# Five stages on one core: tiles shared across stages, inputs loaded a stage ahead, constants in order of need

## The chip, the cores and the metric

The kernel runs on one core of a Trainium2 chip. The metric is the device time of one execution in microseconds (us). The core's engines are TensorE (PE, with its weight loads PEld), VectorE (DVE), ScalarE (ACT), GpSimd (POOL) and SyncE (SP). They run side by side and wait for each other by semaphores. Transfers (DMAs) are issued here by SP, ACT and POOL.

## What is computed

The reference applies two layers to `x` of shape (4, 512, 256). Each layer is an attention and a feed-forward part, each followed by a residual sum and a normalisation:

```python
x = _layernorm(x + _L0_attn_ref(x, ...))   # softmax attention, global and windowed, 16 heads
x = _layernorm(x + _L0_ffn_ref(x, ...))    # 8 routed experts (2 chosen) and a shared one
x = _layernorm(x + _L1_attn_ref(x, ...))   # gated delta rule, 12 heads of 128 keys and 32 values
x = _layernorm(x + _L1_ffn_ref(x, ...))    # 16 routed experts (4 chosen, 128 places each) and a shared one
```

The constants of the kernel (the identity for transposes, masks, triangular matrices, tables for counting) are further inputs.

## The kernel before, in words

`whole_program` (L2663) calls five functions one after the other; each is a stage:

- `layer0_attention` (names `a_`): 4 batches of 512 tokens. For each, PE transposes `x`, projects queries, keys and values, finds the row maxima, scores, weighs and projects out; DVE adds `x` and normalises; POOL stores the result `x1` to HBM.
- `layer0_experts` (`f_`): for each batch, PE transposes `x`, routes, and runs ten hidden units (`hide`) and nine sums (`project`); ACT applies gelu, DVE adds up and normalises, POOL stores `x2`.
- `layer1_projections` (`p_`): gates, decays and values of all tokens. The results that the next stage keeps in SBUF lie in the object `kept` (`hT`, `decays`, `beta`); the gates, the values `v` and the decays `alpha` are stored to HBM by SP.
- `layer1_delta_rule` (`d_`): 12 heads, pipelined. Per head PE projects keys and queries, DVE convolves them, POOL inverts small triangular blocks by substitution, PE and DVE run the recurrence over four chunks, and SP stores the head's output `o_out` to HBM.
- `layer1_output` (`m_`): projects the heads' outputs (`project`), adds `x2`, normalises, routes, runs the shared expert, and then gathers rows for each of 16 experts, multiplies, and scatters them back with addition; a last normalisation makes the output.

A stage allocates its own SBUF tiles, PSUM banks and semaphores, and writes one program for each engine in a `Block`. Each engine works its list in order, waits included. The stage ends when all engines are through their lists; the lists end in waits for the last stores to land (`stored`), as in L475 on POOL:

```python
pool.dma_start(x1_b[b, :, :, :], x1[:]).then_inc(stored, 16)
pool.wait_ge(stored, 16 * BATCH)
```

Then the semaphores are cleared and all engines meet (`clear_and_free_semaphores`, `all_engine_barrier`), and the next stage starts with its loads. What is at the head of each stage:

- Attention: SP issues eleven loads of constants and weights (L151), all counted on one semaphore `loaded`, then `x` of the first two batches (L155). PE, ACT and DVE wait for all eleven (`loaded`, 176) before their first instruction; PE's first work is `turn_x(0)` (L168).
- Experts: SP loads `ident`, `x` of batch 0, the gate's weights (PE and ACT wait for the first and third as `first_in`), then the experts' weights `w1` (L704, L709) with the biases, `w2`, and further `x`. `turn_x(0)` is L727, `hide` is L751; ACT waits for all of `w1` before its first gelu (L816).
- Projections: SP loads `ident`, `x`, the gates' weights, small vectors, the values' weights, and at the end the first two heads' weights for the next stage. `turn_x(0)` is L1060. At the stage's end SP stores `alpha` and the last values (L1036) and waits for both to land.
- Delta rule: POOL fills `U32`, `L32` and `X2` with zeros and three small tiles with constants; PE, ACT and DVE wait for all six (`consts`, 6). SP loads decays, values and gates. PE's first work is `project` (L1468). The last head's output is multiplied by DVE (`finish`, L1934), stored by SP (L1422), and awaited.
- Output: SP loads `ident`, `w_o`, `o` and `x2` of two batches. ACT first issues nine loads (L2293), two stores of zeros (L2296) and two loads of the router's weights, turned, one element at a time (L2299); only then it copies PE's transposes (`project`, L2306). PE transposes `o` in L2124 and projects it in L2133.

## Time and profile before

| | |
|---|---|
| median of 3 runs | 1870.4 us (1864.61 to 1874.24) |
| the profiled execution, its own time | 1870.46 us |
| its span, first to last instruction | 1868.5 us |
| mean granted clock of TensorE | 0.915 of full speed |
| PE, DVE, ACT, POOL busy | 79%, 56%, 35%, 35% of the span |

The stages can be told apart in the timeline by the prefixes of the tiles' names: attention to about 549 us, experts to 737, projections to 823, the delta rule to 1602, the output to the end. A row of the timeline gives the start, the duration, the engine, the line, the operation and the tiles, and in brackets how long the engine had been idle and what it was released by. "SPq" and "ACTq" are issues of transfers, which take time on the issuing engine; the landing is later.

### The profile page before, as it was taken

Reading aid. Unit: us, or ns where it says so; the run is one execution under the profiler, and the core shown is the slowest. Engines: PE = TensorE matmul, PEld = TensorE weight load, DVE = VectorE, ACT = ScalarE, POOL = GpSimd, SP = SyncE. Lnnn points to the kernel's source line nnn. Section 1 sums busy time; section 2 is a strip of 40 time slices with the busy share of each in tenths; the row PEclk is TensorE's granted clock in tenths of the full one; section 3 lists DMA queues with packets and bytes.
Section 4 is the critical chain, followed back from the end, with each engine's and each line's share of the span. In section 5 each row is a group of like instructions: output and inputs, shape, how many; then the busy total and the mean of one; then the engine's idle time right before and its main releaser. Section 6 shows DMA issues by size and latency. Waiting matters only on the chain. (4 is left out here: it accounts for less than half of the span.)

```text
span 1868.5 us, 27548 instructions
## 1 busy us (share of the span) xinstructions
PE 1483.0 (79%) x10473; PEld 1005.7 (54%) x10524; DVE 1054.7 (56%) x2369; ACT 661.6 (35%) x1308; POOL 645.1 (35%) x1037
## 2 busy tenths in 40 slices
PE   4787787786959996857599999999999997387782
PEld 3354554444536664523367666576666686365572
DVE  3846556547123444558477767777777732155553
ACT  3062161341512220534254444554455522022112
POOL 3020020200000000012686666877667762111343
PEclk8999899899979998979799999999999976598897
DMA  1000000000012001341213432223432121421355
GB/s 55 1 1 1 23 2 1 23 1 1 12 39 65 23 12 57 118 121 39 43 34 67 80 80 55 46 60 80 80 75 45 38 43 29 128 97 57 86 118 140
DMA packets 223876, 97.08 MB, mean 52 GB/s; under 512 B 166905, under 2 KB 212386, under 8 KB 223746
## 3 DMA queue, kind: packets, MB, share of 16 engines
q1 hardware_dynamic: 212306, 80.88, 18.1%
q0 software_dynamic: 5376, 12.59, 2.6%
q10 hardware_dynamic: 6064, 1.86, 0.4%
q8 instruction: 83, 1.36, 0.3%
q14 instruction: 47, 0.39, 0.1%
HBM read 63.48 MB, written 31.82 MB: 51 GB/s over the span
## 5 line engine op out<-in xcount | busy, mean ns | idle before, releaser
L1810 DVE SCALAR_TENSOR_TENSOR d_conv<-d_prep,k_cw,d_conv 128x511 f32<-128x511 f32 (+2 forms) x288 | 214.3, 746 | 32.4 <-ACT d_conv L1664 25.6
L1785 POOL TENSOR_TENSOR d_blk<-d_blk,d_prod 64x30 f32<-64x30 f32 (+4 forms) x360 | 201.9, 561 | 28.2
L1468 PE MATMUL d_prep<-k_hT,k_w 128*128 128x512 f32 x384 | 187.7, 613 | 24.7 <-POOL d_power L1762 12.9
L1781 POOL TENSOR_TENSOR d_prod<-d_blk 64x30 f32<-64x30 f32 (+4 forms) x360 | 192.8, 535 | 27.3
L424 ACT ACTIVATE a_probs<-a_acc 128x896 f32<-128x896 f32 x128 | 117.1, 918 | 172.1 <-PE a_acc L248 109.1
L523 DVE TENSOR_REDUCE a_top<-a_turn 128x4 f32<-128x512 f32 (+3 forms) x240 | 147.5, 652 | 48.3 <-PE a_turn L210 40.4
L1497 PE MATMUL d_prep<-d_kq 128*128 128x256 f32 x384 | 101.5, 404 | 48.5 <-DVE d_AT L1853 26.1
L471 POOL TENSOR_TENSOR a_rstd<-a_rstd,a_mhalf 128x4 f32<-128x4 f32 x4 | 4.1, 1027 | 371.2 <-DVE a_rstd L575 371.2
L1664 ACT ACTIVATE d_conv<-d_prep,k_cw 128x512 f32<-128x512 f32 x96 | 66.0, 687 | 134.6 <-PE d_prep L1468 134.6
L1497 PEld LDWEIGHTS d_prep<-d_kq 128*128 128x128 f32 x384 | 68.2, 194 | 84.2 <-DVE d_AT L1853 38.2
L1468 PEld LDWEIGHTS d_prep<-k_hT,k_w 128*128 128x128 f32 x384 | 67.8, 196 | 84.7 <-issue 47.8
L209 PE MATMUL a_turn<-a_kS,a_qS 128*128 128x128 bf16 (+3 forms) x246 | 61.0, 300 | 31.1 <-DVE a_top L523 25.7
L1710 ACT ACTIVATE d_X<-d_rec 32x128 f32<-32x128 f32 (+1 forms) x144 | 43.0, 306 | 116.6 <-PE d_rec L1503 113.6
L892 DVE SCALAR_TENSOR_TENSOR f_y<-f_sum,f_gates,f_y 128x256 f32<-128x256 f32 x128 | 53.1, 478 | 52.7 <-PE f_sum L766 52.6
L766 PE MATMUL f_sum<-f_w,f_h 128*128 128x256 f32 x320 | 78.1, 383 | 0.2 <-DVE f_y L892 0.2
L751 PE MATMUL f_hid<-f_xT,f_w 128*128 128x512 f32 x160 | 77.4, 611 | 0.2 <-ACT f_h L816 0.2
L766 PEld LDWEIGHTS f_sum<-f_w,f_h 128*128 128x128 f32 x320 | 59.7, 190 | 26.6 <-issue 20.8
L457 POOL TENSOR_SCALAR a_stack<-a_parts 128x64 bf16<-128x64 bf16 x128 | 35.1, 308 | 107.9 <-DVE a_parts L508 107.9
L1503 PE MATMUL d_rec<-d_L,d_AT 128*128 128x128 f32 x384 | 49.2, 291 | 26.4 <-DMA d_L<-mid_l_blk 26.4
L1640 ACT ACTIVATE d_kq<-d_conv 128x512 f32<-128x512 f32 x96 | 60.4, 629 | 26.2 <-DVE d_conv L1810 23.5
L1503 PEld LDWEIGHTS d_rec<-d_L,d_AT 128*128 128x128 f32 x384 | 48.8, 207 | 27.7 <-DMA d_L<-mid_l_blk 27.2
L816 ACT ACTIVATE f_h<-f_hid,f_b 128x512 f32<-128x512 f32 x40 | 27.4, 687 | 102.2 <-PE f_hid L751 102.1
(352 smaller groups left out, 3340.8 us busy)
## 6 DMA issues: line engine op xcount, KB each, us to landing
d_alpha<-mid_alpha SPq DMA_DIRECT2D x48, 256.0 KB, 4.0
mid_gate<-p_gate SPq DMA_DIRECT2D x4, 768.0 KB, 3.4
mid_v<-p_v_tok SPq DMA_DIRECT2D x4, 768.0 KB, 3.7
d_v_h<-mid_v SPq DMA_DIRECT2D x12, 256.0 KB, 6.0
d_gate_h<-mid_gate SPq DMA_DIRECT2D x12, 256.0 KB, 5.0
mid_a_blk<-d_AT SPq DMA_DIRECT2D x48, 64.0 KB, 2.6
d_blk<-mid_a_blk SPq DMA_DIRECT2D x12, 256.0 KB, 3.5
mid_l_blk<-d_blkT SPq DMA_DIRECT2D x12, 256.0 KB, 2.9
```

The source lines that it names most:

```text
L209: nc.tensor.matmul(acc, q[:, i * P:(i + 1) * P], k[:, 0:w], start=True, stop=False)
L424: nc.scalar.activation(probs[:, g % 2, h % 4, u, 0:896], AB[u][:].rearrange("p a t -> p (a t)")[:, 0:896], ACT.Exp, scale=A_SCALE).then_in ...
L523: nc.vector.tensor_reduce(dst, src, AX.X, ALU.max).then_inc(maxed, 1)
L751: last = nc.tensor.matmul(HB[unit % 2][:], w1[:, k, n, :], xT[:, b % 2, k, :], start=k == 0, stop=k == CK - 1)
L766: last = nc.tensor.matmul(YB[total_u % 2][:, t, :], h[:, (F_UNITS * b + n) % 4, t * P:(t + 1) * P], w2[:, n, :], start=n == chunks[0], sto ...
L1468: last = nc.tensor.matmul(PB[f % 2][:], w[:, n % 2, i, k, :], hT[:, k, b * T:(b + 1) * T], start=k == 0, stop=k == CK - 1)
L1497: last = nc.tensor.matmul(PB[f % 2][:, 2 * c * P:2 * (c + 1) * P], kq[:, n % KQ_BUFS, 0, b, t0:t0 + P], kq[:, n % KQ_BUFS, :, b, t0:t0 + P ...
L1503: last = nc.tensor.matmul(LB[b][:, c, :], left[:, b * CH + c, :], right[:, b * CH + c, :], start=True, stop=True)
L1664: nc.scalar.activation(conv[:, f % 2, :], PB[f % 2][:], ACT.Copy, scale=cw[:, n % 2, f % 2, TAPS - 1:TAPS]).then_inc(scaled, 1)
L1781: nc.gpsimd.tensor_tensor(pr, blk[:, 0:t, t:t + 1].broadcast_to([lanes, t, m]), blk[:, t:t + 1, t + 1:BLK].broadcast_to([lanes, t, m]), AL ...
L1785: nc.gpsimd.tensor_tensor(blk[:, 0:t, t + 1:BLK], blk[:, 0:t, t + 1:BLK], pr, ALU.subtract).then_inc(subst, 1)
L1810: ins = nc.vector.scalar_tensor_tensor(dst, PB[f % 2][:, 0:T - j], cw[:, n % 2, f % 2, TAPS - 1 - j:TAPS - j], dst, ALU.mult, ALU.add)
```

## The change

Tiles that two or more stages can share are allocated in `whole_program` in three objects: `Carried` (the identity, the gate's weights, `x` of two batches, `x1`, `x2`, for all stages), `Kept` (as before, with more tiles, from the experts on) and `Early` (all that the projections load). A stage loads what the next one needs into them. The last store of a stage counts on a semaphore of these objects, on which the first reader in a later stage waits; the stage itself no longer waits for it. In the attention, the loads are ordered by need and counted on four semaphores. In the delta rule, the zero fills are no longer awaited by all engines; several of its tiles become views of shared ones. In the output, ACT issues nothing, and SP issues all loads. Cut to its core:

```diff
@@ layer0_attention, sync
-            for dst, src in ((ident[:], d["c_ident"]), (identb[:], d["c_identb"]), (rope[:], d["c_rope"]),
...
-                sp.dma_start(dst, src).then_inc(loaded, 16)
-            for b in range(BATCH):
+            def load_x(b):
                 if b >= 2:
                     sp.wait_ge(resid, b - 1)
                 sp.dma_start(x[:, b % 2, :, :], x_b[b, :, :, :]).then_inc(x_in[b % 2], 16)
 
+            sp.dma_start(ident[:], d["c_ident"]).then_inc(ident_in, 16)
+            load_x(0)
+            for dst, src in ((w_qkv[:, :, 0:C], d["L0_attn_wq"].rearrange("(k p) n -> p k n", p=P)),
...
+                sp.dma_start(dst, src).then_inc(qkv_in, 16)
+            sp.dma_start(rope[:], d["c_rope"]).then_inc(rope_in, 16)
+            for dst, src in ((identb[:], d["c_identb"]), (qmask[:], d["c_qmask"]), (kmask[:], d["c_kmask"]),
...
+                sp.dma_start(dst, src).then_inc(loaded, 16)
+            for b in range(1, BATCH):
+                load_x(b)
+            sp.dma_start(carried.w_gate[:], d["L0_ffn_gate_w"].rearrange("(k p) n -> p k n", p=P)).then_inc(carried.gate_in, 16)
+            for b in range(2):
+                sp.wait_ge(stored, 16 * (b + 1))
+                sp.dma_start(carried.x[:, b, :, :], x1_b[b, :, :, :]).then_inc(carried.x_in[b], 16)
@@ layer0_attention, tensor
-            pe.wait_ge(loaded, 176)
+            pe.wait_ge(ident_in, 16)
...
+                if c == 0 and t == 0:
+                    pe.wait_ge(qkv_in, 48)
...
+                if c == 0 and n == 0:
+                    pe.wait_ge(loaded, 96)
@@ layer0_attention, scalar, gpsimd and vector
-            act.wait_ge(loaded, 176)
...
-                pool.dma_start(x1_b[b, :, :, :], x1[:]).then_inc(stored, 16)
-            pool.wait_ge(stored, 16 * BATCH)
+                pool.dma_start(x1_b[b, :, :, :], x1[:]).then_inc(stored if b < BATCH - 1 else carried.x1_out, 16)
+            pool.wait_ge(stored, 16 * (BATCH - 1))
...
-            dve.wait_ge(loaded, 176)
+            dve.wait_ge(rope_in, 16)
@@ layer0_experts
+                    if b == BATCH - 1:
+                        sp.wait_ge(carried.x1_out, 16)
...
-            sp.dma_start(ident[:], d["c_ident"]).then_inc(first_in, 16)
-            load_x(0)
-            sp.dma_start(w_gate[:], d["L0_ffn_gate_w"].rearrange("(k p) n -> p k n", p=P)).then_inc(first_in, 16)
...
-            for b in range(1, BATCH):
+            for b in range(2, BATCH):
                 load_x(b)
+            early.load(sp, d)
+            kept.load(sp, d)
+            for b in range(BATCH - 1):
+                sp.wait_ge(stored, 16 * (b + 1))
+                sp.dma_start(early.x[:, b * NT:(b + 1) * NT, :], x2_b[b, :, :, :]).then_inc(early.x_in[b], 16)
...
-            pe.wait_ge(first_in, 32)
+            pe.wait_ge(carried.gate_in, 16)
...
-            pool.wait_ge(stored, 16 * BATCH)
+            pool.wait_ge(stored, 16 * (BATCH - 1))
@@ layer1_projections, sync
-            sp.dma_start(ident[:], d["c_ident"]).then_inc(first_in, 16)
-            load_x(0)
...
+            sp.wait_ge(carried.x2_out, 16)
+            sp.dma_start(x[:, rows[BATCH - 1], :], x2_b[BATCH - 1, :, :, :]).then_inc(x_in[BATCH - 1], 16)
...
-            sp.wait_ge(stored, 16 * 2 * BATCH)
-            sp.wait_ge(alpha_out, 16)
-            sp.wait_ge(kept_in, 16 * 9)
+            sp.wait_ge(stored, 16 * (2 * BATCH - 1))
+            sp.wait_ge(kept.loaded, 16 * 9)
@@ layer1_delta_rule, sync
+            def load_output():
+                sp.wait_ge(proj, 8 * D_H)
+                sp.wait_ge(stored, 16 * (D_H - 1))
+                o_b = d["o"].rearrange("(b t p) c -> b p t c", p=P, t=NT)
+                for b in range(2):
+                    sp.dma_start(kept.o[:, b, :, 0:VDIM - D_V], o_b[b, :, :, 0:VDIM - D_V]).then_inc(kept.o_in[b], 16)
+                sp.dma_start(kept.w_o, d["L1_attn_Wo"].rearrange("(k p) n -> p k n", p=P)).then_inc(kept.output_in, 16)
...
+                        sp.dma_start(kept.w_route[:, k, :], d["L1_ffn_gate_w"][:, k * P:(k + 1) * P].rearrange("e p -> p e")).then_inc(kept.output_in, 16)
 
+            sp.wait_ge(kept.alpha_out, 16)
             load_decays(0, range(BATCH))
+            sp.wait_ge(kept.values_out, 16)
...
-            sp.wait_ge(stored, 16 * D_H)
+                if n == D_H - 2:
+                    load_output()
@@ layer1_delta_rule, tensor, gpsimd and vector
-            pe.wait_ge(consts, 6)
...
-            for m, value in ((U32, 0.0), (L32, 0.0), (X2, 0.0), (ones, 1.0), (mhalf, -0.5)):
+            for m, value in ((ones, 1.0), (mhalf, -0.5), (power, 0.5)):
                 nc.gpsimd.memset(m[:], value).then_inc(consts, 1)
...
+            pool.wait_ge(kept.values_out, 16)
+            pool.wait_ge(kept.alpha_out, 16)
+            for m in (U32, L32, X2):
+                nc.gpsimd.memset(m, 0.0).then_inc(zeroed, 1)
...
+                    here, there = slice(0, 2 * NT), slice(2 * NT, TILES)
+                    nc.vector.tensor_tensor(o_out[:, there, :], o[:, there, :], mean2[:, there, None].broadcast_to([P, 2 * NT, D_V]), ALU.mult).then_inc(o_done, 1)
+                    nc.vector.tensor_tensor(kept.o.rearrange("p b t c -> p (b t) c")[:, :, VDIM - D_V:], o[:, here, :],
+                                            mean2[:, here, None].broadcast_to([P, 2 * NT, D_V]), ALU.mult)
@@ layer1_output, sync and scalar
+            for b in range(2):
+                sp.dma_start(x2[:, b, :, :], x2_b[b, :, :, :]).then_inc(x2_in[b], 16)
+            for dst, src in ((before[:], d["c_before"]), (ones[:], d["c_ones"]), (w_s[:, :, 0, 0:M_IS], d["L1_ffn_sw_gate"].rearrange("(k p) n -> p k n", p=P)),
...
+                sp.dma_start(dst, src).then_inc(loaded, 16)
+            sp.wait_ge(zeroed, 4)
+            for dst in (d["x3"][TOKENS:, :], d["y"][TOKENS:, :]):
+                sp.dma_start(dst, zeros[:]).then_inc(loaded, 16)
+            sp.wait_ge(kept.last_out, 16)
+            for b in range(2, BATCH):
...
-                act.dma_start(dst, src).then_inc(loaded, 16)
...
-                    act.dma_start(w_route[:, k, :], d["L1_ffn_gate_w"][:, k * P:(k + 1) * P].rearrange("e p -> p e")).then_inc(loaded, 16)
```

In the delta rule `conv` becomes a view of `carried.x1`, `squares` of `carried.x`, `blkT` of `carried.x2`, and `U32`, `L32` and `X2` of `kept.wide`, which is also the projections' `v_tok`; `kept.o`, `kept.w_o` and `kept.w_route` are views of `kept.hT`.

## Rows read from the trace of the kernel before

**Rows 1.** The page, busy time, share of the span and instructions of each engine.

```profile
PE 1483.0 (79%) x10473; PEld 1005.7 (54%) x10524; DVE 1054.7 (56%) x2369; ACT 661.6 (35%) x1308; POOL 645.1 (35%) x1037
```

**Rows 2.** Timeline at the program's start: start us, us, engine, line, operation, tiles.

```profile
1.19 0.42 SPq L151 DMA_DIRECT2D a_identb<-c_identb  x1
...
6.01 1.02 SPq L155 DMA_DIRECT2D a_x<-L_attn_x  x2
...
12.22 1.94 PE L168 MATMUL a_turn<-a_ident,a_x 128*128 128x128 f32 x8 [12.22 <-DMA a_x<-L_attn_x]
```

**Rows 3.** Line L474, the four stores of `x1` by POOL, issue to landing.

```profile
DMA to landing us min/median/max: 3.4/3.4/3.6
```

**Rows 4.** Timeline at the boundary from attention to experts.

```profile
548.95 0.80 POOL L474 DMA_DIRECT2D mid_x<-a_x  x1 [1.99 <-DVE a_x L582]
553.83 0.35 SPq L700 DMA_DIRECT2D f_ident<-c_ident  x1
...
558.37 1.97 PE L727 MATMUL f_turn<-f_ident,f_x 128*128 128x128 f32 x8 [16.11 <-DMA f_w_gate<-L_ffn_gate_w]
...
568.86 1.28 ACT L816 ACT_TABLE_LOAD   x1 [2.18 <-PE f_hid L751]
```

**Rows 5.** Timeline at the boundary from experts to projections.

```profile
735.82 0.79 POOL L844 DMA_DIRECT2D mid_x<-f_x  x1 [1.99 <-DVE f_x L912]
...
745.03 1.94 PE L1060 MATMUL p_turn<-k_ident,p_x 128*128 128x128 f32 x8 [16.25 <-DMA p_x<-mid_x]
```

**Rows 6.** Timeline at the boundary from projections to the delta rule.

```profile
821.73 0.36 SPq L1036 DMA_DIRECT2D mid_v<-p_v_tok  x1
...
832.10 5.24 PE L1468 MATMUL d_prep<-k_hT,k_w 128*128 128x512 f32 x8 [12.94 <-POOL d_power L1762]
...
849.47 3.87 PE L1468 MATMUL d_prep<-k_hT,k_w 128*128 128x512 f32 x8
```

**Rows 7.** Timeline at the boundary from the delta rule to the output.

```profile
1600.75 0.69 DVE L1934 TENSOR_TENSOR d_o_out<-d_o,d_mean 128x512 f32<-128x512 f32 x1 [2.86 <-POOL d_mean L1771]
...
1611.92 11.67 ACTq L2299 DMA_DIRECT2D m_w_route<-L_ffn_gate_w  x2
1612.58 1.94 PE L2124 MATMUL m_hid<-m_ident,m_o 128*128 128x128 f32 x8 [17.28 <-DMA m_o<-mid_o]
1614.31 1.06 PE L2124 MATMUL m_turn<-m_ident,m_o 128*128 128x128 f32 x4
...
1623.64 1.09 ACT L2306 ACTIVATE m_oT<-m_hid 128x512 f32<-128x512 f32 x2 [28.87 <-issue]
...
1625.27 8.04 PE L2133 MATMUL m_sum<-m_w_o,m_oT 128*128 128x256 f32 x24 [9.90 <-ACT m_oT L2306]
```

**Rows 8.** Line L155, the four loads of the attention's `x`, issue to landing.

```profile
DMA to landing us min/median/max: 3.8/4.9/6.9
```

**Rows 9.** Line L709, the loads of the routed experts' `w1`: issues, then landing.

```profile
L709 SPq DMA_DIRECT2D f_w<-L_ffn_w x2: 669/870/1071, 557.2 to 557.9; - x2
...
DMA to landing us min/median/max: 5.3/5.8/6.3
```

**Rows 10.** Busy time in 821 to 822; after the engines: granted clock, DMA share, GB/s.

```profile
821.00:822.00 1.00, 0.00 (x0) 0.00 (x0) 0.00 (x0) 0.71 (x2) 0.00 (x0) 0.79 0.39 96
```

**Rows 11.** Timeline of SP alone, the delta rule's end; two issues merged.

```profile
1554.95 46.96 SPq L1422 DMA_DIRECT2D mid_o<-d_o_out  x2
```

**Rows 12.** Line L2296, the two stores of zeros by ACT, issue to landing.

```profile
DMA to landing us min/median/max: 11.0/11.4/11.8
```

**Rows 13.** DMA queues from 820 to 828 us: packets, MB, share of 16 engines.

```profile
q8 instruction: 1, 0.02, 1.0%
q14 instruction: 1, 0.01, 0.2%
```

**Rows 14.** Lines L1810 and L1236, DVE's convolution steps: ns min/median/max, first and last.

```profile
L1810 DVE SCALAR_TENSOR_TENSOR d_conv<-d_prep,k_cw,d_conv x288: 736/748/751, 836.5 to 1486.9; 128x511 f32<-128x511 f32 x48, 128x509 f32<-128x509 f32 x48, 128x510 f32<-128x510 f32 x48
...
L1236 DVE SCALAR_TENSOR_TENSOR p_conv<-p_val,p_cv_w,p_conv x36: 741/749/752, 767.5 to 817.0; 128x511 f32<-128x511 f32 x12, 128x510 f32<-128x510 f32 x12, 128x509 f32<-128x509 f32 x12
```

More of the change, by code:

```diff
@@ L642, with layer0_experts @@
 SENTINEL = -3.0e38
-def layer0_experts(nc, d):
+def layer0_experts(nc, d, carried, kept, early):
     ctx, sems = ExitStack(), []
@@ L944 @@
 SERIES = 7
+NG = VDIM + 2 * D_H
 def delta_constants():
@@ L953, in delta_constants, with layer1_projections @@
     return out
-def layer1_projections(nc, d, kept):
+def layer1_projections(nc, d, carried, kept, early):
     ctx, sems = ExitStack(), []
@@ L1035, in store_values @@
                 sp.wait_ge(v_out, VC * (b + 1))
-                sp.dma_start(v_b[b, :, :, :], v_tok[:, rows[b], :]).then_inc(stored, 16)
+                sp.dma_start(v_b[b, :, :, :], v_tok[:, rows[b], :]).then_inc(stored if b < BATCH - 1 else kept.values_out, 16)
             for b in range(BATCH + 2):
@@ L1277, in _, with layer1_delta_rule @@
                 convolve(3, m)
-    nc.clear_and_free_semaphores(sems)
+    nc.clear_and_free_semaphores(sems + early.sems)
     nc.all_engine_barrier()
 KQ_BUFS = 3
-def layer1_delta_rule(nc, d, kept):
+def layer1_delta_rule(nc, d, carried, kept):
     ctx, sems = ExitStack(), []
@@ L1305, in sem @@
             return sems[-1]
-        ident, diag = kept.ident, kept.diag
+        ident, diag = carried.ident, kept.diag
         hT, decays, beta, w, cw = kept.hT, kept.decays, kept.beta, kept.w, kept.cw
@@ L1319, in layer1_delta_rule @@
         AT, qkT = sb("AT", [P, 2, TILES, P]), sb("qkT", [P, 2, TILES, P])
-        blk, blkT = sb("blk", [NB * TILES, BLK, BLK]), sb("blkT", [NB * TILES, BLK, BLK])
-        prod = sb("prod", [NB * TILES, BLK * BLK // 4])
-        U32, L32 = sb("U32", [P, TILES, P]), sb("L32", [P, TILES, P])
+        blk = sb("blk", [NB * TILES, BLK, BLK])
+        blkT = carried.x2[0:NB * TILES, :, :].rearrange("p a (b c) -> p (a b) c", c=BLK)
+        prod = kept.small[0:NB * TILES, :]
+        U32, L32, X2 = (kept.wide[:].rearrange("p (n t c) -> p n t c", n=3, t=TILES)[:, n, :, :] for n in range(3))
         U, L = sb("U", [P, TILES, P]), sb("L", [P, TILES, P])
-        X2 = sb("X2", [P, TILES, P])
         X3 = X2
@@ L1421, in store @@
                 sp.sem_inc(sp_carrier)
-                sp.dma_start(o_d[n, :, :, :], o_out[:]).then_inc(stored, 16)
+                if n < D_H - 1:
+                    sp.dma_start(o_d[n, :, :, :], o_out[:]).then_inc(stored, 16)
+                else:
+                    sp.dma_start(o_d[n, :, 2 * NT:, :], o_out[:, 2 * NT:, :]).then_inc(kept.last_out, 16)
+            def load_output():
[5 more added lines that the diff above has]
+                sp.dma_start(kept.w_o, d["L1_attn_Wo"].rearrange("(k p) n -> p k n", p=P)).then_inc(kept.output_in, 16)
+                with nc.allow_non_contiguous_dma(reason="the router's weights, turned"):
+                    for k in range(CK):
+                        sp.dma_start(kept.w_route[:, k, :], d["L1_ffn_gate_w"][:, k * P:(k + 1) * P].rearrange("e p -> p e")).then_inc(kept.output_in, 16)
+            sp.wait_ge(kept.alpha_out, 16)
             load_decays(0, range(BATCH))
+            sp.wait_ge(kept.values_out, 16)
             for n in range(3):
@@ L1997, in expert_constants, with layer1_output @@
     return out
-def layer1_output(nc, d):
+def layer1_output(nc, d, carried, kept):
     ctx, sems = ExitStack(), []
@@ L2062, in layer1_output @@
         w_in = [sem(f"e_w_in{s}") for s in range(2)]
-        o_in, x2_in = ([sem(f"{n}{s}") for s in range(2)] for n in ("o_in", "x2_in"))
+        o_in, x2_in = kept.o_in, [sem(f"x2_in{s}") for s in range(2)]
         x3_stored = sem("x3_stored")
@@ L2671, in whole_program @@
     d["out"] = out.rearrange("b t c -> (b t) c")
-    layer0_attention(nc, d)
-    layer0_experts(nc, d)
     with ExitStack() as ctx:
+        carried = Carried(nc, ctx)
+        layer0_attention(nc, d, carried)
         kept = Kept(nc, ctx, d)
-        layer1_projections(nc, d, kept)
-        layer1_delta_rule(nc, d, kept)
-    layer1_output(nc, d)
+        with ExitStack() as brief:
+            early = Early(nc, brief)
+            layer0_experts(nc, d, carried, kept, early)
+            layer1_projections(nc, d, carried, kept, early)
+        layer1_delta_rule(nc, d, carried, kept)
+        layer1_output(nc, d, carried, kept)
 def kernel(**inputs):
```

215 lines of the change are left out of this document (116 added, 99 removed).

## The prediction

> **What bounds the kernel now.** I read the page's busy line first, then the timeline around the start of the program and around each of the four places where one stage ends and the next begins, and last the landing times of the transfers there. PE is busy for 1483.0 of 1868.5 us [rows 1], so no single resource fills the span; the question is what PE does in the other 385 us. The timelines show five stretches in which every compute engine stands still. At the program's start PE's first matmul comes at 12.22 us, released by the transfer of `a_x` that SP issued at 6.01, behind eleven others [rows 2]. At the first boundary (attention to experts) the last store is issued on POOL from 548.95 to 549.75, lands 3.4 us after its issue [rows 3], and only then the engines meet; SP's first instruction of the new stage is at 553.83, and PE starts at 558.37, after 16.11 us of idleness, when the last of three loads is in [rows 4]. So a boundary has three parts: the wait for the last store (549.75 to 552.35), the meeting itself (552.35 to 553.83, 1.48 us), and the first loads (553.83 to 558.37). The other boundaries have the same parts: PE idles 16.25 us before 745.03 [rows 5], 12.94 us before 832.10 [rows 6], 17.28 us before 1612.58 [rows 7]. The last has a fourth: after its first transposes PE waits again, for ACT, which is stuck in issuing two element-wise loads of the router's weights (11.67 us) and copies at 1623.64 only; PE's first projection runs at 1625.27 [rows 7]. All of this lies on the path, because after each boundary nothing else is running.
>
> **The change, part by part.** Each term is the time at which PE's work starts before, less the time at which it can start after; what follows it in the stage is the same code and moves with it.
>
> *Start.* The tile `x` goes from twelfth to second place in SP's list, behind `ident`; PE waits for these two alone. The second issue was at 1.19 [rows 2]. Loads of `a_x` landed 3.8 to 6.9 us after issue [rows 8]; I take 3.8, since now only 64 KB lie ahead, and keep 4.9 for the range. 1.19 + 3.8 + 0.1 = 5.1 against 12.22: **7.1 us** (bound 6.0). The weights for the first projection follow at some 0.47 us each and have PE's eight transposes, ACT's copies and a table load as cover; if that were gone PE would wait at the projection for at most the difference of their landings, 1 to 2 us. Masks and `w_o` are awaited one step later.
>
> *Attention to experts.* The last store no longer holds POOL, and `ident`, the gate's weights and `x` are already loaded. SP's queue has these extra loads at the end of attention, behind its last `load_x`, where it only waits. New start: 549.75 + 1.48 = 551.23 against 558.37: **7.1 us**. Late next: the experts' weights. SP issued their second half at 557.9, landing at most 6.3 us later, 564.2 [rows 9], that is 10.4 after SP's first issue of the stage. Three issues ahead of it are gone, so at most 551.23 + 10.4 = 561.6. The first to need it is ACT's gelu, at 568.86 before [rows 4], 561.7 after: just covered, without counting the three issues. `load_x(3)` waits for the fourth store; that is long in.
>
> *Experts to projections.* 735.82 + 0.79 + 1.48 = 738.09 against 745.03 [rows 5]: **6.9 us**. `Early.load` and `Kept.load`, 21 issues, sit in SP's queue behind `load_x(3)`, and the three loads of `early.x` behind them each wait for a store. Nothing of the stage is queued there any more, so they cost nothing while experts run; without this cover they would be the loads of now. The fourth `x` load, issued at the stage's start, is needed three batches later.
>
> *Projections to delta rule.* SP's last store ends its issue at 821.73 + 0.36 = 822.09 [rows 6]; start at 823.57. PE no longer waits for POOL's six fills (idle released by `d_power`), so 832.10 becomes 823.57: **8.5 us**. The three big fills now wait for the values' store, and go on beside PE's and DVE's first convolutions; the first who needs them is the gather after the first substitution on POOL itself. SP's new waits for the two stores hold only loads that are used after eight convolutions.
>
> Here the clock matters. PE's first eight matmuls of this stage take 5.24 us, eight like them later 3.87 [rows 6]; the granted clock averages 0.79 in the microsecond from 821, in which PE does nothing [rows 10]: it falls there from 2.4 to 1.2 GHz. So PE would still start at 1.2 GHz at 823.57, and I take no gain. The Trainium skill, "TensorE: Matmul & The Clock Gate", Part 1, says that the lower rate is the default and activity lifts it, so that shorter rests keep an engine fast; by that the term would be 8.5 + 1.4. The trace shows the fall ahead of the new start, so I stay with 8.5.
>
> *Delta rule to output.* `finish` of the last head is split; its first half releases the store. The whole product takes 0.69 us [rows 7], so the store starts at most some 0.3 earlier and the second half ends at most 0.1 later: zero. SP ends its issue at 1601.91 [rows 11], start at 1603.39. PE's twelve transposes take 1612.58 to 1615.37, 2.79 us; ACT's three copies then go at once (1623.64 to PE's 1625.27, 1.63): the projection starts at 1607.81 against 1625.27 [rows 7]: **17.5 us**. The moved loads: `load_output` follows the eleventh head's store, issued at 1554.95 [rows 11]. Its wait for that store, 5 issues and the 11.67 us of the element-wise pair end before 1585, with only the last store behind them at 1601; were it late, PE would wait by that much. ACT's eleven other issues go to SP, ahead of the third batch's `o`; PE asks for them after its second projection, at least 8.04 + 2.79 + 1.63 us after 1607.81, 1620.3. Their issue ends near 1603.4 + 13 x 0.5 = 1609.9; the last two landed up to 11.8 us after issue before, beside the element-wise pair [rows 12]: up to 1621.7. The large `o` loads and that pair are gone from the queue, so I take no wait, and 1.4 for the range.
>
> *Sum.* 7.1 + 7.1 + 6.9 + 8.5 + 17.5 = 47.1. The profiled execution took 1870.46 us (span 1868.5, 2 us around it), the median of the runs is 1870.4: 1870.46 - 47.1 = **1823.4, say 1823 us**.
>
> **The rivals.**
>
> *A. The stores are awaited all the same*, because the meeting itself lets outstanding transfers land. For it: in every boundary before, nothing was outstanding, so the trace cannot exclude it. Against it: the wait that POOL and SP perform is written in the program and is taken out. Each of four boundaries keeps 552.35 - 549.75 = 2.6 us [rows 3, 4]: 10.4 less, 1834 us.
>
> *B. Engines are late after the meeting*, their next code not yet there. Before, PE's, DVE's and ACT's first instructions waited for data, which would have hidden this: at most 553.83 to 558.37, 4.5 us a boundary. Between 820 and 828 one block of instructions moved on each of two instruction queues [rows 13], and SP began 1.48 us after the landing without delay. At half of the bound for four boundaries: 9 more, 1832 us; at the whole, 1841. The Trainium skill, "Runtime: NRT & Kernel Launch", section "Instruction fetch mechanics", says that a sequencer streams its code in order and that a taken branch out of the loaded pages stalls it; stage changes here would be such places if they are branches. No row shows such a stall.
>
> *C. The change does not do what it says*: each first step still waits for some transfer begun inside the stage. Then only the stores' waits are saved, 4 x 2.6: 1860 us. The lists in the diff speak against it; the experts' weights are the one narrow place.
>
> *D. Slower.* Delta-rule tiles move into shared ones (`conv` into `carried.x1`, `U32`, `L32`, `X2` into `kept.wide`). If a tile's place slowed its readers, the 288 convolution steps of DVE (748 ns) would show it first: they decide from 47.1 / 288 = 0.16 us each, 22%; at 25% the time is 1823 + 54 = 1877 us, if all lies on the path. Against it: the same operation on other tiles in the projections takes 741 to 752 ns, here 736 to 751 [rows 14].
>
> **How the numbers follow.** Forecast 0.73 (own range 1815 to 1830: landing of `a_x`, the tail of loads, the clock's phase at five starts, the runs' own spread), A 0.09, B 0.10, C 0.04, D 0.02, the rest unknown. The range 1813 to 1836 takes the forecast, A and the likelier half of B. A change of 0.5%, 9 us, is about what a measurement of this kernel can tell from none: faster holds the forecast, A, B and half of C, 0.95; same 0.03; slower 0.02.
>
> **What would show it.** PE's first matmul near 5 us; its first instructions of the stages about 1.5 us after the last store's issue; PE's rests there 4 to 9 us in place of 13 to 17; ACT's copy at 1606 less what was gained earlier, with no issue ahead of it; the time between two boundaries unchanged. Wrong would be: PE starting some 4 us after SP's last issue (A), engines starting at different times after a meeting (B), a DMA as releaser of a stage's first PE work (C), a longer stretch between boundaries (D).

## The result: 1826.7 us instead of 1870.5, and the profile after

The changed kernel takes 1826.7 us in the median of 4 runs (1823.77 to 1829.13); the kernel before took 1870.53 us beside it (1864.61 to 1874.24). The ratio is 0.9769, with a 95% interval from 0.9745 to 0.9793: 43.8 us less. The forecast was 1823, its range 1813 to 1836. The profiled execution took 1823.77 us, its span is 1822.0 us, 46.5 less than before.

From the page of the changed kernel, the span, the busy line (as [rows 1]), the granted clock by slices, and the group of convolution steps (busy us and mean ns behind the bar; as [rows 14]):

```profile
span 1822.0 us, 27598 instructions
PE 1488.5 (82%) x10524; PEld 1004.0 (55%) x10524; DVE 1058.4 (58%) x2370; ACT 661.9 (36%) x1308; POOL 644.2 (35%) x1037
PEclk8999899899898998989799999999999986698897
...
L1822 DVE SCALAR_TENSOR_TENSOR carried_x<-d_prep,k_cw,carried_x 128x511 f32<-128x511 f32 (+2 forms) x288 | 214.6, 746 | 23.6 <-ACT carried_x L1672 16.7
```

PE's busy time has hardly moved (1483.0 before), so what went is rest. The convolution steps, now on shared tiles, take 746 ns in the mean, as they did on the page before (the 748 of [rows 14] is the median):

```profile
L1810 DVE SCALAR_TENSOR_TENSOR d_conv<-d_prep,k_cw,d_conv 128x511 f32<-128x511 f32 (+2 forms) x288 | 214.3, 746 | 32.4 <-ACT d_conv L1664 25.6
```

The timeline of the changed kernel shows where (start in us, duration, engine and line; in brackets how long the engine had rested and what released it). First the program's start, which answers to [rows 2], and the first boundary, to [rows 4]:

```profile
1.18 0.42 SPq L149 DMA_DIRECT2D a_x<-L_attn_x  x1
5.42 1.94 PE L180 MATMUL a_turn<-carried_ident,a_x 128*128 128x128 f32 x8 [5.42 <-DMA a_x<-L_attn_x]
...
540.36 0.80 POOL L489 DMA_DIRECT2D mid_x<-carried_x  x1 [1.99 <-DVE carried_x L597]
544.89 0.83 SPq L717 DMA_DIRECT2D f_w<-L_ffn_shared_w  x2
544.90 0.10 POOL L854 MEMSET f_mhalf<- 128x4 f32 x1 [3.74 <-POOLq L650]
545.08 1.94 PE L745 MATMUL f_turn<-carried_ident,carried_x 128*128 128x128 f32 x8 [11.39 <-PEq L650]
```

PE starts at 5.42 instead of 12.22 us. At the boundary no transfer releases PE any more; but it starts 3.92 us after the end of POOL's issue (541.16 to 545.08), not 1.48. POOL itself rests 3.74 us at the line of the meeting (`POOLq L650`). The second boundary, against [rows 5], has the same shape; the third and the fourth, against [rows 6, 7], don't:

```profile
722.52 0.79 POOL L864 DMA_DIRECT2D mid_x<-carried_x  x1 [1.99 <-DVE carried_x L932]
726.95 1.94 PE L1051 MATMUL p_turn<-carried_ident,early_x 128*128 128x128 f32 x8 [11.47 <-PEq L952]
...
804.54 0.36 SPq L1030 DMA_DIRECT2D mid_v<-k_wide  x1
806.03 6.50 PE L1476 MATMUL d_prep<-k_hT,k_w 128*128 128x512 f32 x8 [4.07 <-PEq L1270]
808.50 5.29 POOL L1776 MEMSET k_wide<- 128x2048 f32 x3 [2.29 <-issue]
...
1573.93 0.43 DVE L1950 TENSOR_TENSOR k_o_out<-d_o,d_mean 128x256 f32<-128x256 f32 x1 [2.86 <-POOL d_mean L1784]
1574.46 0.37 SPq L1418 DMA_DIRECT2D mid_o<-k_o_out  x1
1576.30 1.94 PE L2151 MATMUL m_hid<-carried_ident,k_hT 128*128 128x128 f32 x8 [7.83 <-PEq L1991]
1579.13 1.09 ACT L2318 ACTIVATE m_oT<-m_hid 128x512 f32<-128x512 f32 x2 [11.19 <-PE m_turn L2151]
1580.76 5.45 PE L2160 MATMUL m_sum<-k_hT,m_oT 128*128 128x256 f32 x24 [1.66 <-ACT m_oT L2318]
```

Where SP issues the last store, PE starts 1.13 us (804.90 to 806.03) and 1.47 us (1574.83 to 1576.30) after the issue's end. That store lands 3.4 to 3.9 us after its issue (L1030) or 2.1 (L1418), so at the third boundary PE is at work before the landing. The zero fills go on beside PE's first matmuls. In the output stage ACT's copies follow PE's transposes at once.

The span's 46.5 us can be accounted for from such rows. The distance from the start of the last store's issue to PE's first matmul fell from 9.42, 9.21, 10.37 and 11.05 us to 4.72, 4.43, 1.49 and 1.84: 27.6 us. The start gave 6.8, and PE's rest ahead of the output's first projection, from 9.90 to 1.66, gave 8.2. That is 42.6; the other 3.9 lie inside the stages (the attention is 1.8 shorter, the output some 2.0 beyond its rest, the delta rule 1.0, the projections 0.9 longer).

### The profile page after: what moved, and what is told of

It reads as the page before. It is cut to its first block and busy times, and to the rows that moved or that the text cites. A ratio compares the mean times of both kernels' runs of the same rounds, so it can differ in the third digit from the quotient of the medians.

```text
span 1822.0 us, 27598 instructions
## 1 busy us (share of the span) xinstructions
PE 1488.5 (82%) x10524; PEld 1004.0 (55%) x10524; DVE 1058.4 (58%) x2370; ACT 661.9 (36%) x1308; POOL 644.2 (35%) x1037
## 5 line engine op out<-in xcount | busy, mean ns | idle before, releaser
L1822 DVE SCALAR_TENSOR_TENSOR carried_x<-d_prep,k_cw,carried_x 128x511 f32<-128x511 f32 (+2 forms) x288 | 214.6, 746 | 23.6 <-ACT carried_x L1672 16.7
L1798 POOL TENSOR_TENSOR d_blk<-d_blk,k_small 64x30 f32<-64x30 f32 (+4 forms) x360 | 201.2, 559 | 28.2
L1794 POOL TENSOR_TENSOR k_small<-d_blk 64x30 f32<-64x30 f32 (+4 forms) x360 | 191.9, 533 | 27.3
L1672 ACT ACTIVATE carried_x<-d_prep,k_cw 128x512 f32<-128x512 f32 x96 | 66.0, 687 | 125.5 <-PE d_prep L1476 125.2
L1718 ACT ACTIVATE k_wide<-d_rec 32x128 f32<-32x128 f32 (+1 forms) x144 | 43.0, 306 | 114.9 <-PE d_rec L1513 112.0
L1648 ACT ACTIVATE d_kq<-carried_x 128x512 f32<-128x512 f32 x96 | 60.4, 629 | 26.8 <-DVE carried_x L1822 24.6
L1513 PE MATMUL d_rec<-k_wide,d_AT 128*128 128x128 f32 x384 | 49.0, 290 | 24.2 <-DMA k_wide<-mid_l_blk 24.2
L1513 PEld LDWEIGHTS d_rec<-k_wide,d_AT 128*128 128x128 f32 x384 | 48.6, 206 | 25.4 <-DMA k_wide<-mid_l_blk 24.8
```

The costliest lines, as they stand in the source:

```text
L1513: last = nc.tensor.matmul(LB[b][:, c, :], left[:, b * CH + c, :], right[:, b * CH + c, :], start=True, stop=True)
L1672: nc.scalar.activation(conv[:, f % 2, :], PB[f % 2][:], ACT.Copy, scale=cw[:, n % 2, f % 2, TAPS - 1:TAPS]).then_inc(scaled, 1)
L1794: nc.gpsimd.tensor_tensor(pr, blk[:, 0:t, t:t + 1].broadcast_to([lanes, t, m]), blk[:, t:t + 1, t + 1:BLK].broadcast_to([lanes, t, m]), AL ...
L1798: nc.gpsimd.tensor_tensor(blk[:, 0:t, t + 1:BLK], blk[:, 0:t, t + 1:BLK], pr, ALU.subtract).then_inc(subst, 1)
L1822: ins = nc.vector.scalar_tensor_tensor(dst, PB[f % 2][:, 0:T - j], cw[:, n % 2, f % 2, TAPS - 1 - j:TAPS - j], dst, ALU.mult, ALU.add)
```

## The experiments

The first question was why PE starts late at the two boundaries where POOL stores.
The table has what the runs' timelines show: PE's first matmul, and from the start of the last store's issue to PE's first matmul of the next stage, at the four boundaries (us).

| run | first matmul | 1 | 2 | 3 | 4 |
|---|---|---|---|---|---|
| before | 12.22 | 9.42 | 9.21 | 10.37 | 11.05 |
| before_again | 12.10 | 9.41 | 9.22 | 10.40 | 11.80 |
| before_start | 5.23 | 9.39 | 9.24 | 10.41 | 11.49 |
| before_fills | 11.49 | 9.32 | 9.45 | 4.90 | 11.16 |
| before_route | 10.90 | 9.42 | 9.37 | 10.37 | 11.50 |
| changed | 5.42 | 4.72 | 4.43 | 1.49 | 1.84 |
| after_again | 5.42 | 4.74 | 4.43 | 1.49 | 1.84 |
| stores_awaited | 5.44 | 5.16 | 4.83 | 4.87 | 3.64 |
| after_x_late | 5.42 | 8.48 | 4.42 | 1.50 | 1.84 |
| sp_last_stores | 5.48 | 1.66 | 1.37 | 1.88 | 1.85 |
| late_clear | 5.90 | 4.03 | 3.88 | 2.14 | 0.96 |
| late_clear_nodrain | 5.39 | 0.55 | 0.40 | 2.18 | 1.03 |
| sp_stores_nodrain | 5.58 | 1.04 | 0.88 | 2.53 | 1.03 |

**sp_last_stores.** SP issues the last `x1` (and, likewise, the last `x2`):

```diff
@@ layer0_attention, sync, at its end
+            sp.wait_ge(ln_done, BATCH)
+            sp.dma_start(x1_b[BATCH - 1, :, :, :], x1[:]).then_inc(carried.x1_out, 16)
@@ layer0_attention, gpsimd
-                pool.wait_ge(ln_done, b + 1)
-                pool.sem_inc(carrier_pool)
-                pool.dma_start(x1_b[b, :, :, :], x1[:]).then_inc(stored if b < BATCH - 1 else carried.x1_out, 16)
+                if b < BATCH - 1:
+                    pool.wait_ge(ln_done, b + 1)
+                    pool.sem_inc(carrier_pool)
+                    pool.dma_start(x1_b[b, :, :, :], x1[:]).then_inc(stored, 16)
```

> The changed kernel with one edit: the last x1 store and the last x2 store are issued by SP, behind its loads, not by POOL. After the change PE starts 3.9 us (541.16 to 545.08) and 3.6 us (723.31 to 726.95) after the end of the last store's issue at the two boundaries where POOL issues it, but 1.13 us (804.90 to 806.03) where SP does. Theory (the meeting lets a store that POOL issued land, and none that SP issued): PE starts 1.1 us after SP's issue, which takes 0.4 instead of 0.8 us, so 2.8 + 0.4 and 2.5 + 0.4 us are gained, 6.1 in all: 1826.7 - 6.1 = about 1820.6 us by the median. Rival (the late start is the fetching of the next stage's code, or another property of these two stages): PE still starts 3.6 to 3.9 us after the issue, 0.4 gained twice, about 1826 us. A second rival (any store of 512 KB is awaited): as the second, with the landing as releaser.

Measured: 1818.23 us median of 5, ratio to before 0.9725 (0.9709 to 0.9741). From its timeline:

```profile
538.24 0.36 SPq L169 DMA_DIRECT2D mid_x<-carried_x  x1
539.70 0.84 SPq L720 DMA_DIRECT2D f_w<-L_ffn_shared_w  x2
539.90 1.94 PE L750 MATMUL f_turn<-carried_ident,carried_x 128*128 128x128 f32 x8 [7.79 <-PEq L653]
```

PE starts 1.30 us after SP's issue ends, while this store lands 2.9 us after its issue's start, at 541.14. The next stage's code is the same, so code that comes late is excluded as the cause, and so is a meeting that awaits every store. The two boundaries gave 3.06 each by the table, 6.1 as expected; the median fell by 8.5 (8.2 by the two ratios to before), more than they account for. Where the rest comes from is not shown.

**stores_awaited.** The waits put back at all four ends:

```diff
+            pool.wait_ge(carried.x1_out, 16)
...
+            pool.wait_ge(carried.x2_out, 16)
...
+            sp.wait_ge(kept.alpha_out, 16)
+            sp.wait_ge(kept.values_out, 16)
...
+            sp.wait_ge(kept.last_out, 16)
```

> The changed kernel with the waits for the last stores put back at the ends of all four stages (POOL waits for x1 and x2, SP for alpha, the values and the last output), and everything else kept. Theory (at POOL's two boundaries the meeting lets the store land anyway, at SP's two it does not): nothing at the first two boundaries, as 3.4 us landing and some 1.2 us of meeting give the 4.7 us that stand there now; at the third 804.54 + 3.6 + 1.2 = 809.3 instead of 806.03, 3.3 us; at the fourth 1574.46 + 2.1 + 1.2 = 1577.8 instead of 1576.30, 1.5 us; sum 4.8: about 1831.5 us. Rival A as predicted (every outstanding store is awaited by the meeting): no change, 1826.7 us. Rival (no store is awaited by a meeting, the late start at the first two boundaries is something else that comes on top): 2.6 us more at each of those too, about 1836.7 us.

Measured: 1834.75 us median of 5, ratio 0.9801 (0.9786 to 0.9816). The boundaries grew by 0.44, 0.40, 3.38 and 1.80 us, 6.0 in all. So the edit that takes away POOL's waits is worth 0.4 us a place, and the same edit at SP's places 3.4 and 1.8: the theory's pattern, with 0.4 where it had nothing. At the third boundary PE now starts 4.51 us after the end of SP's issue (805.98 to 810.49), not 1.13:

```profile
805.62 0.36 SPq L1032 DMA_DIRECT2D mid_v<-k_wide  x1
810.49 6.38 PE L1481 MATMUL d_prep<-k_hT,k_w 128*128 128x512 f32 x8 [7.45 <-PEq L1274]
```

The median is 8.0 above that of the changed kernel; by the two ratios to before it is 6.0, what the boundaries give.

**late_clear.** The semaphores of three stages are cleared later, so that one of the two meetings goes:

```diff
@@ layer0_attention, layer0_experts, layer1_delta_rule
-    nc.clear_and_free_semaphores(sems)
-    nc.all_engine_barrier()
+    LATER.extend(sems)
@@ layer1_projections
-    nc.clear_and_free_semaphores(sems + early.sems)
+    nc.clear_and_free_semaphores(sems + early.sems + LATER)
+    LATER.clear()
...
```

> The changed kernel with the semaphores of a stage no longer cleared at the first, second and fourth boundary but later (at the third and at the end), so that of the two meetings that stand at a boundary the second is gone at these three; POOL's drain in the first meeting stays. The two meetings together take 1.1 us where nothing is awaited (804.90 to 806.03), so one costs some 0.5 us: 3 x 0.5 = 1.5 us less, about 1825 us. Theory (the wait for POOL's store is in the drain of the first meeting): PE starts 3.9 - 0.5 and 3.6 - 0.5 us after POOL's issue. Rival (the wait belongs to the clearing of the semaphores, which POOL does between the two meetings): PE starts about 0.6 us after the issue, 3.3 + 3.0 + 0.5 gained, about 1820 us.

Measured: 1826.04 us median of 5, ratio 0.9757 (0.9744 to 0.9771), not to be told from the changed kernel. PE starts 3.23 and 3.09 us after POOL's issue ends, 0.69 and 0.55 sooner, and 0.88 sooner at the fourth boundary; the third is 0.65 longer. The clearing and its meeting together cost 0.55 to 0.88 us, and the wait for the store is not in them.

**late_clear_nodrain.** In addition, at the ends of the first four stages:

```diff
-        block = ctx.enter_context(nc.Block())
+        block = ctx.enter_context(nc.Block(no_gpsimd_drain=True))
```

> As the run late_clear, and with the meetings at the ends of the first four stages made by semaphores alone, without POOL's drain. The last stores of x1 and x2 are still issued by POOL. Theory (it is this drain that lets POOL's store land): PE starts about 0.6 us after the end of POOL's issue at the first two boundaries, 3.3 and 3.0 us less than in the changed kernel, and 0.5 less at the fourth: 6.8 us, about 1820 us. Rival (POOL is busy with its own transfer, or the next code is late, whatever the drain does): as late_clear, about 1825 us.

Measured: 1820.56 us median of 5, ratio 0.9726 (0.9713 to 0.974). Two timelines of the first boundary decide it. That of late_clear:

```profile
542.89 0.80 POOL L490 DMA_DIRECT2D mid_x<-carried_x  x1 [1.99 <-DVE carried_x L598]
546.73 0.83 SPq L717 DMA_DIRECT2D f_w<-L_ffn_shared_w  x2
546.74 0.10 POOL L854 MEMSET f_mhalf<- 128x4 f32 x1 [3.05 <-POOLq L82]
```

and that of late_clear_nodrain:

```profile
542.16 0.80 POOL L490 DMA_DIRECT2D mid_x<-carried_x  x1 [1.99 <-DVE carried_x L598]
542.52 0.83 SPq L717 DMA_DIRECT2D f_w<-L_ffn_shared_w  x2
542.71 1.94 PE L745 MATMUL f_turn<-carried_ident,carried_x 128*128 128x128 f32 x8 [7.23 <-PEq L82]
542.96 0.12 POOL L854 MEMSET f_mhalf<- 128x4 f32 x1
```

With the drain POOL rests 3.05 us behind its issue, and everybody with it. Without it SP and PE start while POOL's issue still runs, and the rest is gone. The store is POOL's in both, so it is the drain that held it. (The option also turns the meeting into one by semaphores alone, on all engines; SP's run above shows that a meeting with the drain is short when POOL has nothing outstanding.)

**sp_stores_nodrain.** The edits of sp_last_stores and late_clear_nodrain together.

> The edits of sp_last_stores and late_clear_nodrain together: SP issues the last stores of x1 and x2, semaphores are cleared later, and the meetings at the ends of the first four stages are made without POOL's drain. From the last store's issue to PE's first matmul of the next stage it was 1.66, 1.37, 1.88 and 1.85 us at the four boundaries of sp_last_stores (6.8 in all), and 0.55, 0.40, 2.18 and 1.03 (4.2) in late_clear_nodrain. Theory (what the drain costs is only the landing of a store that POOL itself issued, and a dropped meeting gives some 0.6 us): SP's issue of 0.36 us and one meeting, about 1.0 us at the first two, 2.2 and 1.0 at the others, 5.2 in all: about 1 us less than sp_last_stores and 1 more than late_clear_nodrain, so 1817 to 1821 us, not to be told from either. Rival (the gains of the two add up, 8.5 + 6.1 us below the changed kernel, because they come from different places): about 1812 us.

Measured: 1818.97 us median of 5, ratio 0.9729 (0.9713 to 0.9745). The boundaries sum to 5.48 us. The two cures don't add up: they remove one and the same wait.

**before_start.** The kernel before, with the attention's loads in the order and on the semaphores of the change:

```diff
+            sp.dma_start(ident[:], d["c_ident"]).then_inc(ident_in, 16)
+            load_x(0)
...
-            pe.wait_ge(loaded, 176)
+            pe.wait_ge(ident_in, 16)
...
-            act.wait_ge(loaded, 176)
...
-            dve.wait_ge(loaded, 176)
+            dve.wait_ge(rope_in, 16)
```

> The kernel before with one part of the change alone: the attention's loads in order of need, on four semaphores, so that PE waits for ident and x only. Theory (what PE waits for at the start is on the path, and all behind it moves with it): PE's first matmul at 5.4 instead of 12.22 us, as in the changed kernel, 6.8 us gained: 1871.1 - 6.8 = 1864.3 us, and the attention's last store 6.8 us earlier. Rival (the start is given back inside the attention, where the masks, the rotation table or the weights land late): less than 3 us gained, 1868 us or more. Second rival (the attention ends 8.6 us earlier, as the changed kernel's trace shows, so order inside the stage gains more): 1862.5 us.

Measured: 1865.74 us median of 11, ratio 0.9974 (0.9962 to 0.9986): 4.9 us less (2.6 to 7.1), beside 1871.27 for before. PE's first matmul is at 5.23, and the last store at 541.17, which is 7.8 and 6.2 earlier than in the two profiles before (548.95, 547.32). The theory's 6.8 lies in the interval; its rival of under 3 is left only at the edge, and the second one, 8.6, lies outside. How long the attention takes from there varies without any edit to it: from PE's first matmul to the last store it was 536.73 us in before, but 538.24 in before_fills and 533.08 in before_route, which leave that stage alone.

**before_fills.** The kernel before, with the zero fills behind the small constants and awaited by nobody at the start:

```diff
-            pe.wait_ge(consts, 6)
...
-            for m, value in ((U32, 0.0), (L32, 0.0), (X2, 0.0), (ones, 1.0), (mhalf, -0.5)):
-                nc.gpsimd.memset(m[:], value).then_inc(consts, 1)
-            nc.gpsimd.memset(power[:], 0.5).then_inc(consts, 1)
-            pool.wait_ge(consts, 6)
+            for m, value in ((ones, 1.0), (mhalf, -0.5), (power, 0.5)):
+                nc.gpsimd.memset(m[:], value).then_inc(consts, 1)
+            pool.wait_ge(consts, 3)
+            for m in (U32, L32, X2):
+                nc.gpsimd.memset(m[:], 0.0).then_inc(zeroed, 1)
...
```

> The kernel before with one part of the change alone: in the delta rule POOL sets its three small constants first and then fills the three large tiles with zeros, and PE, ACT and DVE no longer wait for the fills before their first instruction. In the profile before, POOL fills from 826.60 to 832.0 and PE starts at 832.10, so PE would start at 826.7. Theory (the start of the delta rule is on the path; of the 8.9 us gained at this boundary 5.4 are the fills and the rest the store that is no longer awaited): 5.4 us gained, about 1865.7 us. Rival (the fills run beside PE's and DVE's first steps and slow them, or POOL is late at its first substitution): under 2 us gained, 1869 us or more.

Measured: 1867.15 us median of 11, ratio 0.9975 (0.9964 to 0.9987): 4.7 us less (2.4 to 6.7), which holds the theory's 5.4 and not the rival. From its timeline, to be read beside [rows 6]:

```profile
824.04 0.36 SPq L1036 DMA_DIRECT2D mid_v<-p_v_tok  x1
828.94 6.43 PE L1469 MATMUL d_prep<-k_hT,k_w 128*128 128x512 f32 x8 [7.48 <-PEq L1279]
829.18 1.80 POOL L1768 MEMSET d_U<- 128x2048 f32 x1
```

The third boundary is 5.47 shorter here, and 3.38 is what the store's wait costs in stores_awaited: 8.85 together, against 8.88 in the changed kernel.

**before_route.** The kernel before, with the two element-wise loads on SP:

```diff
@@ layer1_output, sync
             for b in range(BATCH):
+                if b == 2:
+                    with nc.allow_non_contiguous_dma(reason="the router's weights, turned"):
+                        for k in range(CK):
+                            sp.dma_start(w_route[:, k, :], d["L1_ffn_gate_w"][:, k * P:(k + 1) * P].rearrange("e p -> p e")).then_inc(loaded, 16)
@@ layer1_output, scalar
-            with nc.allow_non_contiguous_dma(reason="the router's weights, turned"):
-                for k in range(CK):
-                    act.dma_start(w_route[:, k, :], d["L1_ffn_gate_w"][:, k * P:(k + 1) * P].rearrange("e p -> p e")).then_inc(loaded, 16)
```

> The kernel before with one part of the change alone: the two element-wise loads of the router's weights are issued by SP, behind the first two batches of the output stage, and no longer by ACT ahead of its first copies. ACT's other issues stay and end at 1611.92, before PE's transposes at 1615.37. Theory (ACT's 11.67 us of issuing is what PE waits for at its first projection): PE's first projection at 1615.4 + 1.7 = 1617.1 instead of 1625.27 us, 8.2 us gained, about 1862.9 us. On the clock: the first projection took 8.04 us before and 5.45 in the changed kernel's profile; if the 9.9 us of rest just before it is the reason, it takes some 5.5 here, 2.5 more gained, 1860.4 us; if it is the 17 us of rest before the transposes, it stays near 8. Rival (SP's queue is held for 11.67 us, and o of the third batch or the router's weights end last): under 4 us gained, 1867 us or more.

Measured: 1862.87 us median of 7, ratio 0.9964 (0.995 to 0.9978): 6.7 us less (4.1 to 9.4), which holds the theory's 8.2 and not the rival of under 4. Its timeline, beside [rows 7]:

```profile
1606.14 13.26 SPq L2085 DMA_DIRECT2D m_w_route<-L_ffn_gate_w  x2
1609.88 1.94 PE L2128 MATMUL m_hid<-m_ident,m_o 128*128 128x128 f32 x8 [17.74 <-DMA m_o<-mid_o]
1612.72 1.08 ACT L2307 ACTIVATE m_oT<-m_hid 128x512 f32<-128x512 f32 x2 [21.10 <-PE m_turn L2128]
1614.34 7.01 PE L2137 MATMUL m_sum<-m_w_o,m_oT 128*128 128x256 f32 x24 [1.66 <-ACT m_oT L2307]
```

The projection follows PE's start by 4.46 us instead of 12.69: 8.2, and SP's 13.26 us of issuing are covered. On the clock neither guess was met: 7.01 us, between 5.5 and 8.

**after_x_late.** The changed kernel, with `x` of the first two batches loaded by the experts themselves:

```diff
@@ layer0_attention, sync
-            for b in range(2):
-                sp.wait_ge(stored, 16 * (b + 1))
-                sp.dma_start(carried.x[:, b, :, :], x1_b[b, :, :, :]).then_inc(carried.x_in[b], 16)
@@ layer0_experts, sync
+            for b in range(2):
+                load_x(b)
```

> The changed kernel with one part undone: x of the first two batches of the experts is loaded at the start of that stage and no longer at the end of the attention; the identity and the gate's weights still come early. Theory (what is loaded ahead is worth the landing of the first load at the stage's start): SP issues x at 544.9, it lands 3.9 us later, PE starts at 548.9 instead of 545.08, 3.8 us lost: 1826.7 + 3.8 = 1830.5 us. Rival (the first load is hidden, because the experts' weights, issued from the stage's start in both, end last and hold PE or ACT): no change, 1826.7 us.

Measured: 1834.67 us median of 5, ratio 0.9802 (0.9789 to 0.9816). From its timeline:

```profile
547.29 0.92 SPq L711 DMA_DIRECT2D carried_x<-mid_x  x2
551.23 1.94 PE L744 MATMUL f_turn<-carried_ident,carried_x 128*128 128x128 f32 x8 [15.15 <-DMA carried_x<-mid_x]
```

The boundary is 3.76 us longer, as the theory said (3.8). The time missed the 1830.5 expected: the median is 8.0 longer, 6.2 by the two ratios to before. The rest isn't at a boundary. In the profile, which is of the slowest of the five executions, it lies in the attention (537.3 us from PE's first matmul to the last store, 534.9 in the changed kernel; there only SP's list is changed), the delta rule (773.1, 768.4) and the output (248.4, 245.7), whose code is not touched. Whether the edit has a part in it is not shown.

**after_again and before_again.** Both kernels unchanged, for the spread.

> The changed kernel once more, unchanged, for the spread of what the other runs are compared with. In the profiles so far the attention took 532.8 to 538.2 us from PE's first matmul to the issue of the last store, and the first projection of the output stage 5.45 to 8.04 us, in kernels whose code there is nearly the same. Theory (these differences come with the execution, by the clock that it is granted, and not from the edits): a second profile of the same kernel differs from the first by 1 to 3 us in the attention, and its boundaries agree within 0.2 us (4.72, 4.43, 1.49 and 1.84); the median is 1825 to 1829 us. Rival (the lengths belong to the program): the attention again takes 534.9 us and the projection 5.45, each within 0.2.

> The kernel before once more, unchanged, for one look. Theory (as for after_again): the boundaries, from the last store's issue to PE's first matmul, again take 9.4, 9.2, 10.4 and 11.1 us within 0.2, and ACT again copies 9.9 us after the transposes, while the attention and the delta rule differ from 536.7 and 769.4 by 1 to 3 us. Rival (the lengths of the stages belong to the program): they agree within 0.3 us, and the 3.9 us that the stages' insides gave in the changed kernel's profile belong to the change.

Measured: 1827.42 us median of 5 for the changed kernel, ratio 0.9776 (0.9759 to 0.9793), and one execution of 1872.68 for the kernel before. The changed kernel's second profile agrees with its first within 0.4 us in every stage (attention 534.74, projection 5.45 again): here the rival holds. But both are of the fastest execution of their runs (1823.77 and 1823.63 us); the others of the same program took up to 1829.13, and no profile shows where. Before's second profile differs by 1.5 us in the attention (535.22) and by 1.35 in the output, as the theory has it; its delta rule agrees within 0.2, as the rival has it, and its fourth boundary is 0.75 longer, where the theory had said 0.2. So the insides of stages move by one to a few us, and how much of that is the execution's and how much the program's stays open.

## Why the prediction was right, step by step

The mechanism held: what stood on the path at the five places was rest, and it went. By the terms of the sum:

- **Start**, 7.1: 6.8 by the trace. PE starts 4.2 us after the issue of `a_x` (1.18 to 5.42), between the two landings named. Alone it is worth 4.9 (2.6 to 7.1). PE's start before was at 10.90 to 12.22 us in the four profiles whose attention is that of before, so up to 1.3 of the 6.8 is the luck of that profile.
- **Attention to experts**, 7.1, and **experts to projections**, 6.9: 4.70 and 4.78. This is the step that failed: "549.75 + 1.48", the meeting's length taken from a boundary at which nothing was outstanding. Rival A was argued down with the wait being written in the program and taken out; but the program has a second wait for the same store, POOL's drain in the meeting. So A was true at the two places where POOL stores, at 2.4 and 2.1 us each, and false at the two where SP does. That is 4.5 us of the 47.1. The prediction's own sign shows it: PE's rests there, 11.39 and 11.47 us, lie above the 4 to 9 that it named.
- **Projections to delta rule**, 8.5: 8.88, of it 5.47 the fills and 3.38 the store.
- **Delta rule to output**, 17.5: 9.21 at the boundary and 8.24 in PE's rest ahead of the projection, 17.45. The queue held: no transfer releases PE there.

So the boundaries gave 42.6 where 47.1 was forecast. The medians differ by 43.8, and the profiled pair by 46.5, near to the forecast only since the insides of stages, which I had put at nothing, gave 3.9 in that pair. That nearness is luck: the profiled execution of the changed kernel is the fastest of its four, and stages whose code was left alone moved by as much in other runs. Of these the output's 2.6 can be seen: its first projection took 5.45 us and not 8.04. The clock granted in that stretch, in the changed kernel, before and in sp_last_stores (window, length, busy times of five engines, then the clock as a share of full speed, the DMA share and GB/s; the first two lines are for the next paragraph but one):

```profile
804.00:806.00 2.00, 0.00 (x0) 0.00 (x0) 0.00 (x0) 0.52 (x2) 0.01 (x1) 0.73 0.46 157
806.00:812.50 6.50, 6.47 (x8) 2.53 (x8) 1.89 (x3) 0.69 (x1) 4.21 (x6) 0.56 1.04 282
...
1580.70:1586.30 5.60, 5.54 (x27) 4.88 (x28) 0.00 (x0) 0.00 (x1) 0.00 (x0) 1.00 1.08 371
```

```profile
1625.20:1633.30 8.10, 8.03 (x26) 6.60 (x27) 0.00 (x0) 0.01 (x1) 0.00 (x0) 0.67 0.05 0
```

```profile
1570.70:1578.20 7.50, 7.50 (x27) 6.26 (x28) 0.00 (x0) 0.00 (x0) 0.00 (x0) 0.73 1.01 349
```

The matmuls ran at 2.4 GHz throughout in the changed kernel, and partly at 1.2 in the others. In sp_last_stores PE rests just as long before them (1.67 us) and they still take 7.43. The shorter rest alone doesn't earn the 2.6.

At the delta rule I took no gain of the clock. The rest fell from 12.94 to 4.07 us, and the first eight matmuls took 6.50 us, 1.26 more than before: the clock averaged 0.73 in the 2 us ahead of PE's start, in which PE did nothing, and 0.56 in the 6.5 us from 806. These rows show the fall ahead of the start, and no 1.4 gained. The Trainium skill ("TensorE: Matmul & The Clock Gate", Part 1) has the lower rate as the default, which activity lifts; the rows agree with that, and the rest of 4.07 us did not keep the engine fast here.

Rival B, late code, is out: PE starts 0.55 us after POOL's issue begins in late_clear_nodrain. The stall that the Trainium skill's "Runtime: NRT & Kernel Launch", "Instruction fetch mechanics", ties to taken branches does not show there; no row tells whether a stage change is such a branch. Rival C is out too: no stage's first PE work is released by a transfer, but the attention's. Rival D is out by the 746 ns of the 288 convolution steps, the same as before.

## What to carry to other kernels

A wait that is taken out of the program helps only if nothing else waits for the same thing: look for what the stage's end does on its own, above all for the engine that issued the last store. Here either cure, the last store on SP or a meeting without POOL's drain, brings the changed kernel to about 1818 to 1821 us, some 0.4% below it; sp_last_stores (0.9725 of the kernel before), late_clear_nodrain (0.9726) and both together (0.9729) can't be told apart. Cost a boundary by its parts (store, meeting, first load, first wait), each from its own rows: the parts of the third boundary, made one at a time, added up to 8.85 of 8.88 us.

## What the runs showed that I had not expected

- A meeting with the drain is not of one length: PE starts 3.6 to 3.9 us after the end of the issue of POOL's 512 KB store, and 1.0 to 1.5 us after that of SP's last store.
- Without the drain, PE starts 0.40 to 0.55 us after the start of POOL's issue, 0.25 us or more before that issue's row ends. The 0.8 us of POOL's issue hold nobody then.
- The third boundary is 0.65 to 1.04 us longer in the three runs that clear three stages' semaphores there (2.14, 2.18, 2.53 against 1.49), but in sp_last_stores, which doesn't, it is 1.88. This was not followed up.
- The same 24 matmuls of the output's first projection took 5.45 us in four of the thirteen profiles (changed, after_again, stores_awaited, after_x_late) and 6.85 to 8.04 in the others. What sets it is open; stores_awaited has the 5.45 although PE rested 9.61 us ahead of its transposes there, and 7.83 in the changed kernel.
